# The Gram stage keeps W by columns, and the second factorisation turns it by 32 columns as it places its right sides

## What is computed

```python
x = x + 0.5 * ffn(layernorm(x))
x = x + attn(layernorm(x))
x = x + 0.5 * ffn(layernorm(x))
# attn: Q, K, V of width 128, then a recursion over the 1024 tokens of each batch
def step(carry, qkv):
    A, M = carry                       # A starts at the identity, M at 0
    q, k, v = qkv
    s_t = sum(k * q)
    u = k / (norm(k) + EPS)
    Au = A @ u
    denom = 1.0 + sum(u * Au)
    A = A - outer(Au, Au) / denom
    M = M + outer(v, s_t * Au / denom)
    return (A, M), M @ q
```

## Time and profile before

| | us |
|---|---|
| median of 3 runs (1150.38 to 1153.01) | 1152.47 |
| the profiled execution | 1156.12 |
| its span, first to last instruction | 1154.4 |
| Gram stage within it (first load issued to the first product of the next stage) | 556.8 to 613.4 |
| second factorisation within it | 613.4 to 816.7 |

### The profile page before, as it was taken

The page is one execution under the profiler, slowest core; times in us unless marked ns, Lnnn a source line. Parts: engine busy times, 40 slices in busy tenths (PEclk is TensorE's granted clock), DMA queues, the critical chain, the costliest instruction groups (busy, mean ns, idle before and its releaser), DMA issues. The chain is left out here.

```text
span 1154.4 us, 28424 instructions
## 1 busy us (share of the span) xinstructions
PE 944.1 (82%) x11460; PEld 726.2 (63%) x11460; DVE 806.3 (70%) x2566; ACT 526.4 (46%) x1083; POOL 300.2 (26%) x254
## 2 busy tenths in 40 slices
PE   3799999999977696778894174783589999999998
PEld 1466767676764576566893153573467777777766
DVE  6777777777648897968367797977266666666663
ACT  4577777777742131312232032110156565655574
POOL 3254443535220000000000000000366454555440
PEclk9899999999998695979798585887699999999999
DMA  5253635355249352334550000055443343433231
GB/s 150 62 128 83 157 100 148 108 139 115 78 138 228 102 133 81 94 102 123 137 165 26 2 4 3 4 149 111 112 118 83 92 101 92 101 92 91 66 74 55
DMA packets 185518, 113.92 MB, mean 99 GB/s; under 512 B 85808, under 2 KB 178352, under 8 KB 184752
## 3 DMA queue, kind: packets, MB, share of 16 engines
q1 hardware_dynamic: 168496, 95.38, 32.4%
q10 hardware_dynamic: 16896, 16.78, 4.7%
HBM read 49.16 MB, written 37.75 MB: 75 GB/s over the span
## 5 line engine op out<-in xcount | busy, mean ns | idle before, releaser
L1651 DVE TENSOR_TENSOR out_h_rest<-out_ps_h,out_h_high 128x512 f16<-128x512 f32 x128 | 88.5, 691 | 100.3 <-ACT out_ps_h L1713 99.7
L1561 POOL TENSOR_TENSOR T<-T,out_bv_rows 128x512 f32<-128x512 f32 x16 | 20.3, 1270 | 483.3 <-DMA out_bv_rows<-in_bqkv 481.6
L1712 ACT ACTIVATE out_h_high<-out_ps_h,b_columns 128x512 f16<-128x512 f32 x128 | 88.2, 689 | 110.8 <-PE out_ps_h L1794 109.7
L393 DVE TENSOR_TENSOR ffn_h_rest<-ffn_ps_h,ffn_h_high 128x512 f16<-128x512 f32 x128 | 87.6, 686 | 67.9 <-ACT ffn_ps_h L565 67.5
L653 PE MATMUL ffn_ps_y<-w_ternary,ffn_h_high 128*128 128x256 f16 x512 | 118.9, 274 | 0.0
L653 PE MATMUL ffn_ps_y<-w_ternary,ffn_h_rest 128*128 128x256 f16 x512 | 118.8, 274 | 0.0
L1806 PE MATMUL out_ps_y<-w_ternary,out_h_high 128*128 128x256 f16 x512 | 118.2, 273 | 0.3 <-DVE out_h_rest L1651 0.3
L1806 PE MATMUL out_ps_y<-w_ternary,out_h_rest 128*128 128x256 f16 x512 | 118.2, 273 | 0.0
L564 ACT ACTIVATE ffn_h_high<-ffn_ps_h,b_columns 128x512 f16<-128x512 f32 x128 | 87.8, 686 | 56.8 <-PE ffn_ps_h L639 56.6
L639 PE MATMUL ffn_ps_h<-ffn_xT_high,w_ternary 128*128 128x512 f16 x256 | 100.8, 394 | 15.1 <-DVE ffn_h_rest L393 10.8
L639 PE MATMUL ffn_ps_h<-ffn_xT_rest,w_ternary 128*128 128x512 f16 x256 | 100.7, 393 | 0.0
(11 more groups left out here) (186 smaller groups left out, 2191.1 us busy)
## 6 DMA issues: line engine op xcount, KB each, us to landing
ffn_x<-in_x SPq DMA_DIRECT2D x16, 512.0 KB, 4.6
x_scratch<-ffn_x_out ACTq DMA_DIRECT2D x16, 512.0 KB, 4.5
aT_scratch<-ffn_aT SPq DMA_DIRECT2D x16, 512.0 KB, 5.3
inv_aT<-aT_scratch SPq DMA_DIRECT2D x16, 512.0 KB, 4.5
T<-x_scratch SPq DMA_DIRECT2D x16, 512.0 KB, 3.8
out_x<-out_x ACTq DMA_DIRECT2D x10, 512.0 KB, 3.3
uT_scratch<-ffn_uT SPq DMA_DIRECT2D x16, 256.0 KB, 5.0
inv_uT<-uT_scratch SPq DMA_DIRECT2D x16, 256.0 KB, 4.4
```

Source lines behind the costliest of these rows:

```text
L393: nc.vector.tensor_tensor(hl[n % 2][:, f], ps_h[f % 3][:], hh[n % 2][:, f], ALU.subtract).then_inc(hl_done, 1)
L1561: nc.gpsimd.tensor_tensor(v0[s], v0[s], bv[:].unsqueeze(1).to_broadcast(group), ALU.add).then_inc(biased, 1)
L1651: nc.vector.tensor_tensor(hl[k % 2][:, f], ps_h[f % 3][:], hh[k % 2][:, f], ALU.subtract).then_inc(hl_done, 1)
L1712: nc.scalar.activation(hh[k % 2][:, f], ps_h[f % 3][:], ACT.Gelu, bias=c.b1[:, f:f + 1])
```

## The change

`gram` no longer turns W. `products` reads W by columns straight from `m.W`, where ScalarE (before: VectorE, into WW) copies each group from `ps_w`. The turn, `ps_u`, WW and `copy_ua` are gone. In the second factorisation the right side of each block is placed by `inject_turned`: for each of the 64 pairs, 32 columns of W are the stationary operand and the identity (128 columns) the moving one, in the order of `tile_order`. `inject` stays for `m.KK`.

```diff
+                def inject_turned(work, r, src, alone):
+                    seen = set()
+                    for p, q in tile_order():
+                        first_in_bank = (p // 4, q) not in seen
+                        seen.add((p // 4, q))
+                        i = nc.tensor.matmul(work[rows_of(q), p, :], src[:, NQ * q + p, block_of(r)], c.ident[:],
+                                             start=first_in_bank, stop=alone, skip_group_check=True)
+                    return i
...
                     if what == "panel right":
                         every = slice(0, P)
-                        i = inject(work, r, m.W, every, every, r == 0)
+                        i = inject_turned(work, r, m.W, r == 0)
...
@@ gram, VectorE
-                def copy_w(st):
-                    v.wait_ge(w_done, st.n + 1)
-                    if not is_first(st):
-                        wait(v, g_done, st.n - 1)
-                        wait(v, u_done, st.n - 1)
-                    nc.vector.tensor_copy(WW[st.s][:], ps_w[st.s][:]).then_inc(W_done, 1)
...
@@ gram, ScalarE
-                def copy_ua(st):
-                    act.wait_ge(u_done, st.n + 1)
-                    nc.scalar.activation(m.W[:, bass.ds(st.n * GROUP, GROUP), :], ps_u[st.s][:], ACT.Copy
-                                         ).then_inc(UA_done, 1)
+                def copy_w(st):
+                    act.wait_ge(w_done, st.n + 1)
+                    nc.scalar.activation(m.W[:, places(st), :], ps_w[st.s][:], ACT.Copy).then_inc(W_done, 1)
                 def step(st):
                     if not is_last(st, NG):
                         copy_a(st.later(1))
-                    if not is_first(st):
-                        copy_ua(st.later(-1))
+                    copy_w(st)
...
@@ gram, TensorE, products
                     if not is_first(st):
                         wait(pe, kk_done, st.n - 1)
-                        wait(pe, UA_done, st.n - 1)
                     for k in range(GROUP):
-                        i = nc.tensor.matmul(ps_g[st.s][:, k], uTb[st.s][:, k], WW[st.s][:, k], start=True, stop=True)
+                        i = nc.tensor.matmul(ps_g[st.s][:, k], uTb[st.s][:, k], m.W[:, bass.ds(st.n * GROUP + k, 1), :],
+                                             start=True, stop=True)
                     i.then_inc(g_done, 1)
-                    for k in range(GROUP):
-                        i = nc.tensor.transpose(ps_u[st.s][:, k], WW[st.s][:, k], c.ident[:])
-                    i.then_inc(u_done, 1)
```

More of the change, by code:

```diff
@@ L1314, in gram, with places @@
         group = [P, GROUP, P]
-        uTa, uTb, Td, A, WW = ([sb(f"{x}{s}", group) for s in range(2)]
-                               for x in ("uT_for_w", "uT_for_g", "Td", "A", "W"))
-        ps_a, ps_w, ps_g, ps_u = (psum(x) for x in ("ps_a", "ps_w", "ps_g", "ps_u"))
+        uTa, uTb, Td, A = ([sb(f"{x}{s}", group) for s in range(2)] for x in ("uT_for_w", "uT_for_g", "Td", "A"))
+        ps_a, ps_w, ps_g = (psum(x) for x in ("ps_a", "ps_w", "ps_g"))
         ua_in = [sem(f"uT_for_w_in{s}") for s in range(2)]
         ub_in = [sem(f"uT_for_g_in{s}") for s in range(2)]
-        td_done, a_done, A_done, w_done, W_done, g_done, kk_done, u_done, UA_done = (
-            sem(x) for x in ("td_done", "a_product", "A_done", "w_product", "W_done", "g_product", "kk_done",
-                             "u_turned", "UA_done"))
+        td_done, a_done, A_done, w_done, W_done, g_done, kk_done = (
+            sem(x) for x in ("td_done", "a_product", "A_done", "w_product", "W_done", "g_product", "kk_done"))
+        def places(st):
+            return bass.ds(st.n * GROUP, GROUP)
         with nc.Block() as block:
@@ L1370, in step @@
                         scale(st.later(2))
-                    copy_w(st)
                     if not is_first(st):
@@ L1395, in step @@
                         copy_a(st.later(1))
-                    if not is_first(st):
-                        copy_ua(st.later(-1))
+                    copy_w(st)
                 copy_a(Step(0, 0))
                 steps(act, NG, step)
-                copy_ua(Step(NG // 2 - 1, 1))
             @block.tensor
```

## The result

| kernel | median us | executions |
|---|---|---|
| before | 1153.45 (1149.22 to 1156.95) | 20 |
| the change | 1161.99 (1152.52 to 1166.03) | 20 |

The ratio of the means is 1.0063, with a 95% interval of 1.0044 to 1.0082: slower by 0.63%, about 7 us (8.5 between the medians), where 1149.8 and at most 1153.0 were forecast. The profiled execution took 1165.64 us (span 1163.9), 9.5 us more span than the one of before. The ratios in this document leave out executions in a slower state, over 1.5% above the quickest of the same kernel, which touches only four of the twelve of e6.

What follows compares the result with a forecast made beforehand. TensorE was taken to bind the Gram stage, its load chain close behind, and VectorE's chain the second factorisation. Gains 1.9 + 0.8 = 2.7 us, zero from the placement: 1152.47 - 2.7 = 1149.8 us, range 1146.0 to 1153.0.

Steps and rivals of the forecast that it cites:

- The start: Gram stage: times_u of group 3 still waits until 571.3 for its load; wait grows from 1.05 to about 2 us, no gain.
- the landing: Gram stage: time from a times_u load's issue until it has landed, taken as 3.14 us in the loop.
- The loop: Gram stage: the chain of loads closes over two groups in 6.08 us, 3.04 a group; gain 1.9 us up to times_u(15).
- rival A: Gram stage: loads keep their old beat, loop 6.24 us, gain some 1.9 us, total 1150.6; chance 0.22.
- The end: Gram stage, last times_u to next stage: 3.9 us instead of 4.76 as two turns and a copy go; gain 0.8 us.
- rival D: Second factorisation: turned placements do not run four strips wide, 17.3 us beyond the cover, total 1167.1; chance 0.05.
- rival C: Gram stage: the longer stop at the start lets TensorE's clock fall, 1.5 to 3 us lost, 1151.3 to 1152.8; chance 0.08.
- 96 more records x 27 ns = 2.6 us at most; I take 1: Second factorisation: stops for code from each placement's 128 instead of 32 records, at most 2.6 us, taken as 1.
- So zero on the path: Second factorisation: the denser placements and their code stay under cover and add zero to the kernel's time.
- The cover of 4.80 us: Second factorisation, third block: TensorE's wait for the turned factors, 4.80 us, hides the longer placement behind VectorE's chain.
- The cover of 12.8 us for the store of W: Second factorisation, fourth block: SyncE's store of W, issued from 785.42, has 12.8 us until the last store at 809.46.
- bounds 0 and, with the cover gone, the excess: Second factorisation: limits on the placement's cost, from 0 to whatever exceeds the 4.8 us cover.

Runs made afterwards that it cites:

- e6: The changed kernel with 32 needless records in the first block and KK loaded as early as before: 1160.2 us (median of eight), ratio 1.0046 to the kernel before.
- e1: The changed Gram stage with the old placement of the right side, W not turned anywhere: 1151.59 us, ratio 0.9976 to the kernel before.
- e3: The changed kernel with the load of KK issued only behind the placement of the fourth block: 1154.08 us, ratio 1.0007 to the kernel before.
- e7: The changed kernel with the fourth block's right side alone placed the old wide way, unturned: 1157.11 us, ratio 1.0031 to the kernel before.
- e9: The changed kernel run again unaltered, for a second trace: 1164.55 us.
- e10: The changed kernel run a third time unaltered, for another trace: 1168.81 us.
- e4: The changed kernel with the late KK load of e3 and 32 needless records in the first block: 1152.68 us, ratio 0.9982 to the kernel before.
- e2: The kernel before, still turning W in the Gram stage, with the new placement `inject_turned`: 1166.24 us, ratio 1.0099 to the kernel before.
- e5: The changed kernel with the late KK load of e3 and 64 needless records in the first block: 1160.4 us, ratio 1.0054 to the kernel before.
- e8: e4 with the Gram stage's load_a of group n+2 issued ahead of load_b of group n+1: 1147.37 us, ratio 0.9938 to the kernel before.
- e11: The kernel before with the Gram stage's load order of e8: 1150.99 us in a single execution, beside 1157.4 of the kernel before.

## Why the prediction was wrong, point by point

**The Gram stage: sum right in the first trace, terms traded.** Forecast 2.7 us, measured 56.59 - 53.90 = 2.69, and in e1 the ratio 0.9976. That close a fit is luck. In the nine traces with this Gram stage (after, e1, e3 to e7, e9, e10) it lasts 53.90 to 55.73 us, median 54.3, so the gain is 0.9 to 2.7 us against the 56.59 of before. And the terms were off in both directions:

- The start was put at no gain and a wait of 2 us. times_u(3) started 570.25 - 557.49 = 12.76 us after the first load, before 571.32 - 556.82 = 14.50. A gain of 1.74 us, and a wait of 0.38. I took the landing for fixed. The load left 9.25 us after the first one instead of 9.45, but its reader started 570.25 - 566.74 = 3.51 us behind it instead of 571.32 - 566.27 = 5.05.
- The loop was put at 6.08 us. It took 6.27, 6.25, 6.13 and 6.20, nearly rival A's 6.24. In the first of them: products 580.43, load_b 1.09 later (581.52), load_a 0.93 later (582.45), times_u 3.26 later (585.71), products 0.99 later (586.70). Two terms were short: the landing by 0.09, and the group behind a wait, which takes 0.99 us and not 0.89. times_u(3) to times_u(15) gained 37.33 - 36.16 = 1.17 us instead of 1.9.
- The Trainium skill (DMA: Bandwidth & Descriptors, Anatomy of one DMA) gave an estimate of 2.6 us for 256 KB on its software path, and with it a loop of 5.54. The loads here, from SyncE's queue and with two in flight, do not agree with it: their medians are 2.9 and 3.1 us.
- The end was put at 3.9 us and took 611.39 - 606.41 = 4.98, more than the 4.76 of before. Products(15) waited 0.73 us for its load, which left at 606.38, 1.09 behind products(13) (605.29), and took 2.8. My chain for the end had only TensorE's and VectorE's work in it; "the end hangs on no load" was wrong.

**Of the second factorisation** these held: 128 records in 3.70 us at the full clock (forecast 3.4 and a tail), so no rival D; 7.82 us of idle time before the fourth block; no fall of the clock in the Gram stage (0.95 over it, 0.94 before, and 1.00 from 571 us on in both), so no rival C.

**The step that failed** is "96 more records x 27 ns = 2.6 us at most; I take 1", with "So zero on the path" behind it. The term itself, the 1 us taken for code, came out as two stops of 1.73 and 1.57 us in the third block and two of 2.00 and 2.43 in the fourth, on the path. I treated code as a supply with a mean rate, whose stops eat into a cover of idle time. The runs show three things in its place.

- Stops do not fall where there is time. They fall where sections end. 96 more records, and the turns removed, move all later ends, and in the third block one came to lie in `finish_diagonal`, on VectorE's chain. The cover of 4.80 us is in front of these products and doesn't help them. Price 3.5 us here, and 3.0 in e3 against e4 (from the turned factors to the next take 707.56 - 698.52 = 9.04 and 710.30 - 704.24 = 6.06).
- The idle time doesn't fetch code. In the earlier trace rows TensorE waits 4.80 us and then runs 128 records whole, and I read this as the wait having filled the store. It had been 69 records into its section.
- The rate is not 27 ns a record beside other traffic. In the fourth block, with the KK load at a DMA share of 1.04, two sections came 768.21 - 762.31 = 5.9 us and 775.52 - 768.21 = 7.3 us apart. The reduction uses 128 records in 5.9 us and can live with that; the narrow placement uses them in 3.6. I had the load at 759.33 in the trace of before, and didn't ask what would run beside it.

**The price of (b)** is mostly not the stops. They are 2.00 + 2.43 = 4.4 us; the half clock costs 337 x (83 - 46 ns) = 12.5. With the 0.6 by which the placement starts later (764.69 against 764.06) these make 17.5 of the 18.0. I had the fall of the clock as a rival, but in the Gram stage; the earlier trace rows showed it between two stops in this very factorisation. The cover of 12.8 us for the store of W was right as a number, but had no room for the 3.3 us of `dinv` stores, which now stand between the two stores of W: 18.04 + 0.79 for a longer issue + 3.4 - 12.85 = 9.4, as measured.

**Range and chances.** The one rival slower than the kernel before (D) was a mechanism that the rows spoke against, with 0.05; "bounds 0 and, with the cover gone, the excess" gave the code no share in the range, though I could name no rule for where its stops fall. An effect with an unknown place belongs in the range with its price on the path: two stops of 2 us would have moved the upper end to 1157.

**Shown and open.** Shown: the loss is the placement's (e1, e2); (a) hangs on where sections end (e4, e5, and the packets); (b) on narrow placement and KK load together (e3, e7, and the packets); the Gram stage was left bound by the order of its loads (e8). Argued only: that the fall of the clock in (b) comes from the stops. Each fall stood behind one (0.80 to 2.94 us in the change, e2, e3, e6, e9, e10), and where the reduction ran whole (before, e1, e4, e5, e7, e8, e11) it took 17.7 to 18.2 us. But the first stop in the change, 2.00 us, left the clock at 1.00 and the 0.80 us of e3 did not, so the length of a stop does not decide it; no run lowers the clock in the reduction without a stop there, or keeps it at 1.00 behind one. Not tried: a wait of TensorE between the 33rd and the 43rd record of a section. Open: why a quarter of the executions of the change are quick, and whether the places of their stops or their clock differ.

## What to carry to other kernels

A change in the number of TensorE's instructions moves every later place where code must be fetched, so check which of the chain's short dense runs a stop can fall into, and count on idle time as cover for code only where TensorE is well into a section (here, 43 of 128 records or more). Before making a stretch denser in instructions, look at what DMA traffic runs beside it. And where an engine's time is taken off a loop, look at once at the order in which its loads are issued: here this was worth another 5 us (e4 against e8).

## What the runs showed of the hardware

- TensorE's code came in packets of 16 KB, 128 matrix records each, one ahead. The next was fetched only when more than 33 and at most 43 records of the present one had run; a wait of 5.7 to 34 us (e5) ahead of that fetched nothing, and a stop of 1.5 to 2.3 us followed (e3, e2).
- From the start of the packet's transfer, which took 1.2 us, to the end of the stop passed 2.6 us (after) and 2.9 us (e2). Beside DMA at 293 GB/s the packets started 3.3 and 4.6 us into the section before, instead of 1.3 (e3), and sections came 5.9 and 7.3 us apart.
- A product of 128 rows by 32 columns with 128 moving cost 3.70 us for 128 (29 ns each), four strips side by side; as turning placement it does the work of 32 records of 512 columns in the same time (3.64 us).
- The granted clock, once at 0.50, stayed there through the 26.7 to 29.5 us that the rest of the fourth reduction took (after, e2, e6, e9, e10), TensorE busy nearly all of the time with products on 32 x 32 tiles; the same products before kept 1.00.
